# Two-layer model on 16 batches: w1's group 0 split and stored within the first pair, and the order of the loads at that pair's end

## The reference

```python
# layer 0, language_ids = itok_B_0_8
h = relu(einsum('bsh,bha->bsa', x, W1[lang]) + b1[lang])        # 512 -> 128
a = x + einsum('bsa,bah->bsh', h, W2[lang]) + b2[lang]          # 128 -> 512
x = x + layernorm(a) * gamma[lang] + beta[lang]
# layer 1, indices = itok_B_0_7
h = gelu(einsum('bni,ih->bnh', x, W1) + b1)                     # 512 -> 2048
x = x + concat(einsum('bnh,ho->bno', h, W2) + b2,               # 2048 -> 384, shared
               einsum('bnh,bhp->bnp', h, We[expert]) + be)      # 2048 -> 128, per batch
```

## Time and profile before

| what | value |
|---|---|
| median of 3 runs | 1427.04 us (1427.02 to 1428.19) |
| the profiled execution's own time | 1427.37 us |
| its span | 1425.5 us |
| PE busy | 1415.2 us, 99% of the span |
| DVE, ACT, POOL busy | 1011.3, 522.9, 653.1 us |
| the first pair's last group ends, the second pair's first product starts | 193.39 us |
| TensorE clock granted | 1.00 in every stretch shown |

### The profile page before, as it was taken

How to read it: one execution, slowest core, us unless ns; L and a number is a source line. 1 busy time by engine, 2 the same in 40 slices (tenths; PEclk the granted TensorE clock), 3 DMA queues, 4 the chain that set the end, 5 groups by cost and what they waited for, 6 DMA issues and landing times.

```text
span 1425.5 us, 18906 instructions
## 1 busy us (share of the span) xinstructions
PE 1415.2 (99%) x6220; PEld 1163.0 (82%) x6220; DVE 1011.3 (71%) x1645; ACT 522.9 (37%) x842; POOL 653.1 (46%) x644
## 2 busy tenths in 40 slices
PE   9999999999999999999999999999999999999999
PEld 6877878888888888888888888888888888888887
DVE  6999895776857867668677676767767687654434
ACT  4743444223442325332253323433234322432231
POOL 5987375451563514734157332564325633351101
PEclk9999999999999999999999999999999999999999
DMA  8646898457865677566774667746787457654332
GB/s 277 248 146 215 223 346 282 160 175 183 279 229 173 177 199 275 198 200 182 204 281 171 211 170 242 255 152 206 199 252 258 148 180 207 202 204 163 133 111 89
DMA packets 273957, 292.39 MB, mean 205 GB/s; under 512 B 129602, under 2 KB 230722, under 8 KB 265796
## 3 DMA queue, kind: packets, MB, share of 16 engines
q1 hardware_dynamic: 264068, 188.15, 43.9%
q10 hardware_dynamic: 9792, 103.03, 19.1%
HBM read 238.70 MB, written 52.43 MB: 204 GB/s over the span
## 4 chain that ended last, share of the span: by engine, by line
PE 89%; POOL 5%; DVE 3%; issue 2%; ACT 1%; SPq 0%; DMA 0%; DVEq 0%; ACTq 0%; POOLq 0%
PE down L275 15%; PE down L277 15%; PE down L276 15%; PE up_b L276 5%; PE up_b L275 5%; PE up_b L277 5%; PE up_c L275 4%; PE up_c L276 4%; PE up_c L277 4%; PE up_a L276 4%; PE up_a L277 4%; PE up_a L275 4%; POOL resid L1344 1%; PE aux L277 1%; PE aux L276 1%
## 5 line engine op out<-in xcount | busy, mean ns | idle before, releaser
L275 PE MATMUL down<-w,g 128*128 128x512 f32 x1024 | 399.0, 390 | 1.4 <-issue 0.6
L276 PE MATMUL down<-w,g 128*128 128x512 f32 x1024 | 398.7, 389 | 0.0
L277 PE MATMUL down<-w,g 128*128 128x512 f32 x1024 | 398.6, 389 | 0.0
L1361 POOL CAST w<-w_raw 128x256 fp32r<-128x256 f32 x125 | 70.6, 565 | 521.1 <-DMA w_raw<-m_we 521.1
L880 DVE TENSOR_TENSOR g<-g_raw,g 128x512 fp32r<-128x512 f32 x256 | 232.9, 931 | 80.0 <-ACT g L661 80.0
L275 PEld LDWEIGHTS down<-w,g 128*128 128x128 f32 x1024 | 192.3, 188 | 42.7 <-issue 1.7
L276 PEld LDWEIGHTS down<-w,g 128*128 128x128 f32 x1024 | 192.4, 188 | 39.7
L277 PEld LDWEIGHTS down<-w,g 128*128 128x128 f32 x1024 | 192.2, 188 | 39.8
L875 DVE TENSOR_TENSOR g_raw<-up_b,s 128x512 f32<-128x512 f32 x63 | 43.5, 691 | 183.0 <-PE up_b L277 170.0
L661 ACT CAST g<-g_raw 128x512 fp32r<-128x512 f32 x256 | 159.0, 622 | 8.0
L653 ACT ACTIVATE g_raw<-up_a,m_b_sb 128x512 f32<-128x512 f32 x64 | 44.1, 689 | 318.6 <-PE up_a L277 318.6
(11 more groups left out here) (225 smaller groups left out, 2506.7 us busy)
## 6 DMA issues: line engine op xcount, KB each, us to landing
w<-w_kept ACTq DMA_DIRECT2D x55, 1792.0 KB, 7.5
w<-w_kept SPq DMA_DIRECT2D x56, 768.0 KB, 5.0
w_raw<-m_we SPq DMA_DIRECT2D x128, 128.0 KB, 4.6
out<-resid SPq DMA_DIRECT2D x64, 256.0 KB, 4.4
xTs_raw<-xT SPq DMA_DIRECT2D x56, 256.0 KB, 3.0
xs<-x SPq DMA_DIRECT2D x56, 256.0 KB, 7.0
w_kept<-w SPq DMA_DIRECT2D x8, 1792.0 KB, 8.0
x_turned<-turned SPq DMA_DIRECT2D x112, 128.0 KB, 3.3
```

What stands on the lines that cost most here:

```text
L275: eng.matmul(bank, a_hi, b_hi, start=opens, stop=False, skip_group_check=True)
L276: eng.matmul(bank, a_hi, b_lo, start=False, stop=False, skip_group_check=True)
L277: return eng.matmul(bank, a_lo, b_hi, start=False, stop=closes, skip_group_check=True)
L1361: eng.tensor_copy(hi, values).then_inc(pool_eh[b], 1)
```

## The change

Group 0 of w1 is finished and stored inside the first pair, and loaded back in finished form at its end.

- Early in the pair SP stores the three plain blocks of group 0 that are ready (`keep_first_w1`, 2 DMAs, 0.79 MB). `load_w1_raw(2)` waits for them.
- In step 4 SP loads group 0's raw blocks again into spare tiles (`load_parts`, 2 DMAs of 0.26 MB, over t1 and b12). In step 5 POOL makes the four sums (`pool_first_sums`), in step 6 ACT casts them (`act_sums_hi`, 128x1024) and POOL subtracts (`pool_sums_low`, 128x1024). In step 6 SP stores them (`keep_sums`, 4 DMAs, 1.05 MB together).
- In step 7 the raw load of group 0, POOL's four sums and its `pool_first_w1_lo(2)`, ACT's `act_w1_hi(8)`, DVE's `dve_rest_w1_lo` and the store `keep_w1(8)` are gone. ACT issues `load_w1` for the second pair's group 0 behind the casts of B11.
- SP's order in step 7: the blocks' loads follow each other, and the raw w2 of group 7 is loaded before group 6 of w2 is stored.
- DVE's order changes: in steps 3 and 4 one `dve_g_lo` each moves from before `dve_sum_u2` to later, in step 3 `dve_w2_lo(2)` goes before `dve_sum_c22`, in step 6 `dve_turns` goes before `dve_w1_lo(7)`, in step 7 `dve_b_lo` of B11 goes behind the two sums.

```diff
     def pe_p1(eng, i, m, k):
-        if i is pairs[1] and k == 0:
-            eng.wait_ge(pool_w1, 3)
-        elif i is not first:
-            eng.wait_ge(in_w1[k % 2], i.count(8 * GROUPS, 16 * (k // 2 + k % 2) - 8 * GROUPS))
+        if i is not first:
+            eng.wait_ge(in_w1[k % 2], i.count(8 * GROUPS, 16 * (k // 2 + 1) - 8 * GROUPS))
...
+    def act_sums_hi(eng):
+        eng.wait_ge(pool_w1, 6)
+        eng.copy(sums_hi[:, :, :], sums[:, :, :]).then_inc(act_first_w, 1)
...
                 for c in range(2):
                     act_block_hi(eng, m, B11, c)
-                if i is not first:
-                    load_w1(eng, m, 0)
+                load_w1(eng, m, 0)
         act_g(eng, i, k, C11)
-        if i is first:
+        if i is first and k < GROUPS - 1:
             act_w1_hi(eng, k + 1)
...
-        if k > 2:
+        if k > 3:
             dve_g_lo(eng, i, k - 1, C12)
-        if k > 3:
+        if k > 4:
             dve_g_lo(eng, i, k - 1, C22)
...
         if k == GROUPS - 1:
-            dve_rest_w1_lo(eng)
+            for c in range(2):
+                dve_b_lo(eng, m, B11, c)
...
+    def pool_first_sums(eng):
+        p11, p12, p21, p22 = (parts[:, n, :] for n in range(4))
+        s4, s1_, s2_, s3_ = (sums[:, n, :] for n in range(4))
+        eng.wait_ge(in_first_w, 48)
+        eng.tensor_tensor(s1_, p21, p22, ALU.add).then_inc(pool_w1, 1)
...
+    def pool_sums_low(eng):
+        eng.wait_ge(act_first_w, 3)
+        eng.tensor_tensor(sums_lo[:, :, :], sums[:, :, :], raw(sums_hi[:, :, :]), ALU.subtract).then_inc(pool_w1, 1)
...
+    def keep_sums(eng):
+        eng.wait_ge(pool_w1, 7)
+        for part, source in ((HI, sums_hi), (LO, sums_lo)):
+            eng.dma_start(raw(w1_kept[0, :, part, S4, :]), raw(source[:, 0, :])).then_inc(kept_first, 16)
+            eng.dma_start(raw(w1_kept[0, :, part, S1:S3 + 1, :]), raw(source[:, 1:4, :])).then_inc(kept_first, 16)
...
     def load_w1(eng, i, k):
-        eng.wait_ge(kept_w1[k % 2], 8 * GROUPS)
+        if k == 0:
+            eng.wait_ge(kept_first, 96)
+        eng.wait_ge(kept_w1[k % 2], 16 * (GROUPS // 2 - 1 + k % 2))
         eng.wait_ge(pe_p[4], seven(i, k - 1))
...
                 if k == GROUPS - 1:
-                    first_w2(eng, k, experts)
+                    load_w2_raw(eng, k)
+                    load_experts(eng, k, experts)
+                    keep_w2(eng, k - 1)
                     keep_w1(eng, k)
...
         if i is first:
             keep_w2(eng, GROUPS - 1)
-            keep_w1(eng, GROUPS)
```

More of the change, by code:

```diff
@@ L94, in build @@
     t1 = sb("t1", [P, 2, TOK])
+    sums_hi = sb("sums_hi", [P, 4, 2 * P], f32r, "t1")
+    sums_lo = sb("sums_lo", [P, 4, 2 * P], f32r, "b12")
+    parts = sb("parts", [P, 4, 2 * P], f32, "t1")
+    sums = sb("sums", [P, 4, 2 * P], f32, "b12")
     s1, u2, q = (sb(n, [P, TOK]) for n in ("s1", "u2", "q"))
@@ L799, in act_step @@
         act_first_sum(eng, i, k)
+        if i is first and k == 6:
+            act_sums_hi(eng)
         if i is first and k % 2 == 1:
@@ L1135, in dve_first_step @@
                 dve_t1(eng, m, c)
+        if k > 2:
+            dve_sum_c12(eng, i, k)
+        if k == 3:
+            dve_w2_lo(eng, k - 1)
+        dve_sum_c22(eng, i, k)
+        if k == GROUPS - 1:
             for c in range(2):
                 dve_b_lo(eng, m, B11, c)
[L1138 to L1143, removed]
-            dve_rest_w1_lo(eng)
         dve_g_lo(eng, i, k, C11)
@@ L1155, in dve_first_step @@
             dve_g_lo(eng, i, k - 1, C22)
+        if k == 4:
+            dve_g_lo(eng, i, k - 1, C22)
+        if k == 6:
+            dve_turns(eng, m, 1, 2)
         if k < GROUPS - 1:
             dve_w1_lo(eng, k + 1)
-            if k == 6:
-                dve_turns(eng, m, 1, 2)
+            if k == 3:
+                dve_g_lo(eng, i, k - 1, C12)
             if k == 5:
@@ L1420, in pool_first_step @@
             return
+        if k == 6:
+            pool_sums_low(eng)
         pool_roots(eng, m, k)
@@ L1519, in load_first_aw @@
         halves = slice(0, D // 2), slice(D // 2, D)
-        for s, landed in zip(halves, (in_aw[0][0], in_first_aw)):
+        for s, landed in zip(halves, (in_aw[0][0], in_first_w)):
             eng.dma_start(aw_tile(first, 0, 0)[1][:, LO, s], a_w1[language, :, s]).then_inc(landed, 16)
@@ L1588, in keep_w1, with keep_first_w1, load_parts @@
         eng.wait_ge(dve_w1, k)
-        if k == GROUPS:
-            eng.wait_ge(pool_w1, 3)
-        eng.dma_start(raw(w1_kept[k % GROUPS, :, :, :, :]), raw(w1[:, k % 2, :, :, :])).then_inc(kept_w1[k % 2], 16)
+        eng.dma_start(raw(w1_kept[k, :, :, :, :]), raw(w1[:, k % 2, :, :, :])).then_inc(kept_w1[k % 2], 16)
+    def keep_first_w1(eng):
+        eng.wait_ge(pool_w1, 2)
+        for of in (slice(A11, A12 + 1), slice(A22, A22 + 1)):
+            eng.dma_start(raw(w1_kept[0, :, :, of, :]), raw(w1[:, 0, :, of, :])).then_inc(kept_first, 16)
+    def load_parts(eng):
+        eng.wait_ge(dve_t, T_ORDER.index((T3, 1)) + 1)
+        eng.wait_ge(pool_tlo, T_ORDER.index((T1, 1)) + 1)
+        for n, of in enumerate((0, GROUPS)):
+            eng.dma_start(parts[:, 2 * n:2 * n + 2, :], m_w1[of, :, :].rearrange("p (a n) -> p a n", a=2)).then_inc(in_first_w, 16)
+    def keep_sums(eng):
[3 more added lines that the diff above has]
+            eng.dma_start(raw(w1_kept[0, :, part, S1:S3 + 1, :]), raw(source[:, 1:4, :])).then_inc(kept_first, 16)
     def load_w1(eng, i, k):
-        eng.wait_ge(kept_w1[k % 2], 8 * GROUPS)
+        if k == 0:
+            eng.wait_ge(kept_first, 96)
+        eng.wait_ge(kept_w1[k % 2], 16 * (GROUPS // 2 - 1 + k % 2))
         eng.wait_ge(pe_p[4], seven(i, k - 1))
```

41 lines of the change are left out of this document (24 added, 17 removed).

## The result

The changed kernel takes 1433.44 us (median of 6, 1432.41 to 1434.57) against 1427.60 us (median of 6, 1427.02 to 1428.19) of the kernel before on the same chip: ratio 1.0041, 95% interval 1.0028 to 1.0054. It is slower, by 5.8 us or 0.4%. I had forecast 1428.7 in a range from 1425.0 to 1431.2.

What follows compares the result with a forecast made beforehand. PE bounds it, busy 1415.2 of 1425.5 us. Product 7 +1.8 us later, less 0.1 of the first pair's gain, gives span 1427.2; from the profiled execution 1429.1, median 0.33 below: 1428.7, range 1425.0 to 1431.2.

Steps and rivals of the forecast that it cites:

- K: First pair's end: landing of the store of w1's group 7, 196.5 us before, forecast 201.3, between 198.8 and 202.4.
- the transfers' main term: Transfers ahead of K at the first pair's end: +5.75 us of added bytes less deductions, +4.8 on K.
- the rival that K comes later still: Pair's end: K beyond 202.4, at 203.5, product 7 at 213.6, +4.0 us, time 1431.0; chance 22%.
- Stores of the sums: Group 0's sums stored ahead of K: 1.05 MB, adding 2.55 us to the transfers.
- The raw loads' going: Raw loads of group 0 no longer ahead of K: 0.52 MB less, -1.3 us.
- Group 0's load: ACT's load ahead of K: 1.84 MB at 411 GB/s, +4.5 us, its large packets served before SP's; landing near 191.
- the two deductions of 0.45 and 0.5: Taken off K's delay: 0.45 us of SP waiting for PE, 0.5 us for the first pair's earlier DVE work.
- the time of w2: Group 7's w2 at the pair's end: ACT's cast starts near 194.7 us, DVE's L1071 successor near 195.5.
- the first pair's gain: Steps 3 and 4: DVE's new order removes three small waits, 0.4 to 0.8 us; 0.1 us survives in the sum.
- VectorE's list decides: Rival at the pair's end: K below 199.5, transfers don't decide, about 1.4 us gained, 1425.6; chance 20%.
- the smooth end: Rival: B22, B21 and w2 not held back, loss of 4.56 us shrinks to about 1, 1422.8; chance 10%.
- my two signs of error: Pair's end: group 7's store landing before 199 us, or PE waiting at 193 us for group 0.

Runs made afterwards that it cites:

- e12: The changed kernel unaltered, timed and profiled a second time; ratio 1.0040 to the kernel before.
- e2: Changed kernel without the four stores of group 0's sums, group 0 loaded from group 2's place (timing only); ratio 1.0021 to the kernel before.
- e4: Kernel before with only VectorE's changed order of low parts and turns in steps 3, 4 and 6 of the first pair; ratio 1.0002.
- e6: Changed kernel with group 0's load on SyncE's queue behind B21 instead of on ScalarE's; ratio 1.0039 to the kernel before.
- e9: Changed kernel with only w2 of group 7 and its experts issued ahead of B22 and B21; ratio 1.0039 to the kernel before.
- e1: Changed kernel with ScalarE's load of w1's group 1 issued behind the copy s and the casts of B21 and T2; ratio 1.0015 to the kernel before.
- e10: Changed kernel, w2 of group 7 ahead of B22 and B21, group 1's load behind copy s and casts of B21, T2, T3, B22; 1426.94 us, ratio 0.9994.
- e7: Changed kernel, w2 of group 7 ahead of B22 and B21, group 1's load behind copy s and casts of B21 and T2; ratio 1.0010 to kernel before.
- e11: e10 with the store of w1's group 7 ahead of the store of w2's group 6; ratio 0.9995 to the kernel before.

## Why the prediction was wrong

**The chain was right.** I had said that the copy s waits for the store of group 7 (K) and that product 7 follows K + 10.1 as soon as K passes 199.5. It followed at K + 10.46 in the first profile and K + 10.43 in e12. Group 0, which I had near 191, landed at 194.86, and product 1 stood at 194.91, just in time (in e12 it waited 0.65 us). The four low parts took 6.86 us beside POOL, as I kept them. My ground for that was read loosely: POOL's two operations of the earlier trace rows start 2.2 us ahead of VectorE's four, not with them.

**The step that failed is the transfers' main term, +4.8 us on K.** With the starts taken off, K was 204.1 in the first profile and 204.6 in e12, so +7.6 to +8.1. My point for it was 201.3 and its upper bound 202.4; the rival that K comes later still had 203.5 and 22%, and even that was short. By parts:

- Stores of the sums, +2.55: right. Between the kernel before and e12 B11's landing moved by 2.7 us (181.13 to 183.34, and 0.5 of start), and without the stores (e2) it is back.
- The raw loads' going, -1.3: between the landings of B11 and B12 lay 4.2 us before and 2.3 in e12, 1.9 less. The 0.6 beyond my term come back in the next point.
- Group 0's load, +4.5, and the two deductions of 0.45 and 0.5: here it failed. From B12's landing to K it was 11.20 us and is 18.44, 7.24 more where I had 3.55. The windows of the kernel before, the whole and its part behind B21's landing, the last number GB/s:

```profile
185.30:196.50 11.20, 10.97 (x49) 8.76 (x47) 11.20 (x11) 6.35 (x10) 9.23 (x7) 1.00 1.02 366
188.60:196.50 7.90, 7.67 (x34) 6.01 (x32) 7.90 (x7) 4.95 (x9) 7.33 (x5) 1.00 0.96 381
```

And of e12, the whole and its parts ahead of and behind B21's landing:

```profile
185.61:204.05 18.44, 14.97 (x58) 11.66 (x57) 8.85 (x11) 5.90 (x9) 6.92 (x6) 0.91 1.01 359
185.61:196.15 10.54, 9.89 (x44) 7.87 (x43) 4.79 (x6) 2.48 (x4) 3.05 (x2) 1.00 0.99 323
196.15:204.05 7.90, 5.07 (x16) 3.78 (x15) 4.06 (x5) 3.41 (x5) 3.87 (x4) 0.78 1.04 407
```

All of the 7.24 us lie between the landings of B12 and B21 (3.30 us before, 10.54 now), where group 0's load passes; from B21's landing to K it is 7.90 us in both. 366 GB/s in 11.20 us are 4.10 MB, 359 in 18.44 are 6.62: 2.52 MB more, where I had counted 1.84. And they run at 359, in the part with the load at 323, not at the 411 GB/s of large packets alone. 1.84 MB at 359 are 5.1 us, and the other 0.68 MB 1.9 us. What these are can be worked out from the packets of the two windows, first before, then e12:

```profile
DMA packets 2781, 4.10 MB, mean 366 GB/s; under 512 B 135, under 2 KB 2528, under 8 KB 2653
DMA packets 3765, 6.61 MB, mean 359 GB/s; under 512 B 169, under 2 KB 3387, under 8 KB 3509
```

825 more packets have from 512 to 2047 bytes. With 512 bytes (the x blocks and the experts) and 1536 (w2) as the sizes there, 0.68 MB makes that an estimated 250 of w2 and 570 of the blocks. The 250, some 0.38 MB, are the store of w2's group 7: it is issued behind the awaited store, at 195.72, 0.8 us before K, in the kernel before, and at 199.09, 5.0 us before K, in e12. It shows in e12's last 3 us before K, where 250 of 437 packets have from 512 to 2047 bytes, while the awaited store has 14336 (the row of all transfers, 201 to 204.05 us):

```profile
DMA packets 437, 1.14 MB, mean 373 GB/s; under 512 B 30, under 2 KB 280, under 8 KB 402
```

The 570, some 0.29 MB, are blocks that in the kernel before had passed by B12's landing, so they are the other side of the 0.6 us above. No run moves the store of w2's group 7 alone, so what it costs is not shown, only that its bytes pass there.

The two deductions did not show. SyncE's wait of 0.4 us for PE is gone, but in its place SyncE waits 1.2 us, ahead of B12's loads, for the stores of transposed x to land, since the raw loads no longer lie between them. From SyncE's waits in e12:

```profile
SPq L1680 <- DMA x_turned<-turned: 1.2, 1, 1.2
```

And the first pair's 0.4 us did not reach B12 in e4 either. That the extra is bytes, and not which queue is served first, is what e6 shows.

**The second step that failed is the time of w2.** I had its cast near 194.7 and L1071's successor at 195.5, inside the shadow of the copy's wait. They were at 198.77 and 199.64 (197.3 and 198.1 with 1.52 of start taken off). TensorE's down product, which I had let start without a wait, waited 3.4 us. The cause is the same: w2 stands right behind B21, and B21's landing, which I had some 5 us later (4.5 less 1.3 plus 1.8), moved by 8.1 us in e12 with the start taken off (188.60 to 196.15). While K holds the copy this costs little: e9 removes it and wins 0.3 to 0.7. But it is a second gate that keeps e1 at 1.0015, and the clock fell to 0.50 during its wait.

**The sum,** K + 10.1 with the K of the runs, gives product 7 at +4.6 to +5.1, and measured are +5.0 and +5.4. Another 0.5 us arises at the next down product, which waits 0.79 us for VectorE's sums instead of 0.29, since these now come behind a chain that is late as a whole. I had written that the down product moves by the same. What stays of the first pair's gain is zero (e4), where I had left 0.1.

**The rivals.** That VectorE's list decides (20%) and the smooth end (10%) are refuted: VectorE stood idle for 7.34 and 3.06 us. e10 shows what they would have needed: no needed operation behind the load of group 1, and w2 ahead of the blocks; then VectorE's list does decide, for 1.1 us. Of my two signs of error the first (the store landing before 199) did not come. The second (PE waiting for group 0 near 193 us) came in e12, with 0.65 us at 193.9, and not in the first profile. Both looked for a load that is cheaper or later than thought, and none for one that is dearer. The rival that K comes later still had the right direction and the failed term, but its K of 203.5 was short too, by 0.6 to 1.1 us.

## What to carry to other kernels

A DMA issue that waits for a landing makes its engine's whole list wait: before bytes are added ahead of that landing, move the issue behind the operations that the critical chain needs (e10 got 6.6 to 7 us back net, 6.3 by the medians, from moved issues alone, with all of the added traffic in place). When transfers are the term, price what is added at the rate of a stretch with the same mix of packets (323 to 366 GB/s here against 411 for large packets alone), and look at what is queued behind the awaited transfer, since part of it passes before its last packet. And look at the next gate: here there were two, and moving one alone gave 3.1 to 3.5 us (e1) or 0.3 to 0.7 (e9), moving both out of the way nearly 7.

## What the runs showed of the hardware

TensorE's granted clock is 1.00 (2.4 GHz) in the stretches shown of the kernel before. In the changed kernel it fell to 0.50 (1.2 GHz) for 6.8 us, from 199.93 us, during a wait of 3.4 us, with matmuls every 0.43 us instead of 0.227. In e7 it fell behind waits of 2.2 and 1.1 us. In e11 it fell behind waits of 0.5, 0.3 and 1.2 us; in the profiled executions of e10 and of the kernel before nearly the same waits left it at 1.00. So a wait can cost more than itself: 1.9 us in e7, 1.1 in e11. It is not the kernel alone that decides: of the 27 executions of the kernel before that were timed beside e11, 19 had a mean clock of 1.000 and a median of 1427.40 us, and 8 had 0.998 or 0.999 and a median of 1428.58. Which waits bring it on stays open.

SyncE's issue of B22 and B21 took 7.28 us for four transfers while ScalarE's queue held the engines, and everything behind in SyncE's list was issued later by that. In the kernel before the same four took 3.46:

```profile
180.78 3.46 SPq L1647 DMA_DIRECT2D xTs_raw<-x_turned  x4
```

Two queues with work passed the same number of packets (82 and 82 in e10), so that the one with the larger packets moved 1.18 MB and the other 0.05.
